# A graph attention layer and a normalised adjacency layer on one core: panel loads out of the attention, two panels' sums beside the first layer, and two re-orderings

## The reference, cut to what matters

```python
# x: 2048 x 512 f32, adj: 2048 x 2048 f32 of zeros and ones, H = 16 heads of 32
seq = (x @ W_seq).reshape(N, H, DH)
score1, score2 = einsum('nhd,d->hn', seq, a1), einsum('nhd,d->hn', seq, a2)
scores = leaky_relu(score1[:, :, None] + score2[:, None, :], 0.2) + (1 - adj) * -65500.0
hidden = einsum('hij,jhd->ihd', softmax(scores), seq).reshape(N, D)
x = layernorm(x + elu(hidden @ W_out + b_out))          # first layer
A = (adj + adj.T) * 0.5 + I;  d = rowsum(A) ** -0.5
y = (adj @ (d[:, None] * A * d[None, :])) @ x
x = layernorm(x + y)                                     # second layer
```

## Time and profile before

| | |
|---|---|
| median of three runs | 788.12 us (787.64 to 789.85) |
| profiled execution, its own time | 786.61 us |
| span of the profiled execution | 784.8 us |
| mean granted TensorE clock | 0.992 |
| TensorE busy | 749.7 us, 96% |
| VectorE, ScalarE, GpSimd busy | 554.7, 409.9, 130.1 us |
| attention, first matmul to last | 88.3 to 489.7 us |
| first layer, to the last `y_part` | 489.7 to 583.5 us |
| `y_product` | 583.5 to 666.4 us |
| `o_product` and end | 668.5 to 784.8 us |

### The profile page before, as it was taken

How to read it: one execution, slowest core, us unless ns; L and a number is a source line. 1 busy time by engine, 2 the same in 40 slices (tenths; PEclk the granted TensorE clock), 3 DMA queues, 4 the chain that set the end, 5 groups by cost and what they waited for, 6 DMA issues and landing times.

```text
span 784.8 us, 29353 instructions
## 1 busy us (share of the span) xinstructions
PE 749.7 (96%) x13731; PEld 552.4 (70%) x13731; DVE 554.7 (71%) x799; ACT 409.9 (52%) x302; POOL 130.1 (17%) x142
## 2 busy tenths in 40 slices
PE   6999799988999999999999999999999999999997
PEld 2444699988999999999999999444434444444443
DVE  2887899998988999999999983687772211333233
ACT  2874887986977888788897880333321111000000
POOL 0000113012320211101111001364433100000000
PEclk9999799999999999999999999999999999999999
DMA  7992510255313111011110121599119800001111
GB/s 304 413 406 103 235 57 5 84 110 110 56 60 84 58 58 36 26 58 58 58 58 4 58 71 31 97 186 175 54 31 172 119 0 1 18 36 41 41 40 41
DMA packets 17770, 71.65 MB, mean 91 GB/s; under 512 B 2016, under 2 KB 2016, under 8 KB 13408
## 3 DMA queue, kind: packets, MB, share of 16 engines
q1 hardware_dynamic: 13040, 52.99, 17.7%
q0 software_dynamic: 4608, 16.78, 14.1%
HBM read 77.89 MB, written 8.65 MB: 110 GB/s over the span
## 4 chain that ended last, share of the span: by engine, by line
PE 78%; DVE 15%; issue 5%; ACT 1%; DMA 1%; POOL 0%; DVEq 0%; POOLq 0%; SPq 0%; ACTq 0%
PE bank L631 13%; PE bank L534 12%; PE bank L533 12%; PE bank L531 11%; PE bank L618 11%; PE bank L467 7%; PE bank L579 7%; DVE RZ L852 5%; PE bank L587 3%; DVE RG L871 2%; DVE RG L867 2%; DVE RP L816 1%; PE bank L571 1%; DVE MT L892 1%; DMA RZ<-in_L_gnn_W_seq_dram 1%
## 5 line engine op out<-in xcount | busy, mean ns | idle before, releaser
L531 PE MATMUL bank<-RP,RG 128*128 128x66 f16 x4096 | 388.8, 193 | 6.9 <-DVE RG L871 3.6
L534 PE MATMUL bank<-RP,MT 128*128 128x66 f16 x4096 | 388.7, 194 | 3.6 <-issue 3.6
L531 PEld LDWEIGHTS bank<-RP,RG 128*128 128x128 fp8e4 x4096 | 386.3, 98 | 8.3 <-DVE RG L871 3.6
L533 PE MATMUL bank<-RP,RG 128*128 128x66 f16 x4096 | 388.7, 195 | 2.1 <-issue 2.1
L534 PEld LDWEIGHTS bank<-RP,MT 128*128 128x128 fp8e4 x4096 | 386.4, 98 | 3.2 <-issue 3.2
L533 PEld LDWEIGHTS bank<-RP,RG 128*128 128x128 fp8e4 x4096 | 386.4, 97 | 2.7 <-issue 2.7
L689 ACT ACTIVATE RZ<-RZ,TAB 128x2048 int8<-128x2048 f32 x160 | 306.6, 1988 | 15.3 <-DVE RG L867 14.5
L852 DVE TENSOR_SCALAR RZ<-RZ,TAB 128x2048 int8<-128x2048 f32 x96 | 132.3, 1378 | 0.0
L867 DVE TENSOR_TENSOR RG<-RZ,MT 128x512 int32<-128x512 int32 x160 | 121.7, 760 | 0.1
L631 PE MATMUL bank<-RZ,MT 128*128 128x512 f16 x512 | 110.7, 379 | 2.2 <-DVE MT L1023 2.2
L391 POOL TENSOR_TENSOR RP<-SEQ,TAB 128x528 f32<-128x528 f32 x32 | 52.2, 1652 | 331.8 <-DVE RP L818 256.7
(11 more groups left out here) (103 smaller groups left out, 593.2 us busy)
## 6 DMA issues: line engine op xcount, KB each, us to landing
RG<-in_adj_t_dram SPq DMA_DIRECT2D x16, 1024.0 KB, 10.6
RZ<-s_rows_dram SPq DMA_DIRECT2D x16, 1024.0 KB, 5.8
seq_copy_dram<-SEQ SPq DMA_DIRECT2D x1, 4224.0 KB, 14.2
S2Q<-in_adj_p_dram POOLq DMA_DIRECT2D x8, 512.0 KB, 6.3
S2Q<-in_adj_tp_dram POOLq DMA_DIRECT2D x8, 512.0 KB, 11.3
RZ<-in_x_dram SPq DMA_DIRECT2D x16, 256.0 KB, 3.5
RP<-in_adj_p_dram POOLq DMA_DIRECT2D x8, 512.0 KB, 7.1
RP<-in_adj_tp_dram POOLq DMA_DIRECT2D x8, 512.0 KB, 13.8
```

What stands on the lines that cost most here:

```text
L531: mm(pb[bank][:, c:c + 2 * DV], step, high, start=(j == 0 and i % IB == 0), stop=(j == NT - 1), skip_group_check=True)
L533: mm(pb[bank][:, c:c + 2 * DV], step, low, start=False, stop=(j == NT - 1), skip_group_check=True)
L534: last = mm(pb[bank][:, c + DV:c + 3 * DV], mask, edge, start=False, stop=(j == NT - 1), skip_group_check=True)
```

## The change

`NE` = 2 panels' sums are made beside the first layer, not `NQ` = 4; their transfers are issued when TensorE is two tiles from the end of the last head. No panel is loaded during the attention. The other fourteen panels go through `y_product`. Panels 2 to 9 are loaded from GpSimd's first-layer loop. The broadcast of score1 comes in `NS` = 4 pieces, each when the same quarter of the masks of the head before is made. `take_back` goes ahead of `low_z`. The first two output tiles leave the products with the last tile of z until both have done the other fifteen.

```diff
-            with sp.Fori(1, H // 2) as p:
-                for u in range(2):
-                    h = p * 2 + u
-                    sp.wait_ge(z_ready, h * NV - NV)
-                    sp.wait_ge(g_ready, h * NT - NT)
-                    load_s1(h, u)
+            def load_s1(h, q):
+                i = slice(q * (N // NS), (q + 1) * (N // NS))
+                sp.dma_start(S1B[:, h % 2, i], s1_rows[h:h + 1, i].broadcast_to([P, N // NS])).then_inc(s1b_in[h % 2], 16)
+            for h in range(2, H):
+                sp.wait_ge(z_ready, (h - 1) * NV)
+                for q in range(NS):
+                    sp.wait_ge(g_ready, (h - 1) * NT + q * (NT // NS))
+                    load_s1(h, q)
...
             for h in range(2, H):
                 prep(h)
-                if 3 <= h < 3 + NQ:
-                    load_panel(h - 3)
-                if 4 <= h < 4 + NQ:
-                    add_panel(h - 4)
-                if 5 <= h < 5 + NQ:
-                    add_diagonal(h - 5)
...
+            gp.wait_ge(g_used, NG + H * NT - 2)
+            for t in range(NE):
+                load_panel(t)
+            for t in range(NE):
+                add_panel(t)
             gp.wait_ge(att_end, 1)
             for t in range(NT):
-                if t < NP:
-                    load_panel(NQ + t)
-                if 2 <= t < 2 + NP:
-                    add_panel(NQ + t - 2)
-                if 4 <= t < 4 + NP:
-                    add_diagonal(NQ + t - 4)
+                if t + NE < NQ + NP:
+                    load_panel(t + NE)
+                if NE <= t < NQ + NP:
+                    add_panel(t)
+                if 2 <= t < 2 + NE:
+                    add_diagonal(t - 2)
+                if 3 + NE <= t < 3 + NQ + NP:
+                    add_diagonal(t - 3)
                 rstd_of(t, var_done, rstd_done)
                 if t + 2 < NT:
                     x_minus_1(t + 2)
-            for t in range(NQ + NP, NT):
-                gp.wait_ge(y_ps, NQ if t < 2 * NQ + NP else t - NQ - NP + 1)
-                load_panel(t)
-            for t in range(NQ + NP, NT):
-                add_panel(t)
-            for t in range(NQ + NP, NT):
-                add_diagonal(t)
+            for t in range(NQ + NP, NT + 2):
+                if t < NT:
+                    gp.wait_ge(y_ps, t - NQ - NP + 1)
+                    load_panel(t)
+                if NQ + NP < t <= NT:
+                    add_panel(t - 1)
+                if NQ + NP + 1 < t:
+                    add_diagonal(t - 2)
...
-                for i in range(NQ):
+                for i in range(NE):          # y_part
...
-                    pe.wait_ge(s2_done, NQ)
+                    pe.wait_ge(s2_done, NE)
...
-            for t in range(NQ, NT):
+            for t in range(NE, NT):
                 y_product(t)
             pe.wait_ge(mt_back, NT)
-            for t in range(NT):
-                o_product(t)
+            for t in range(2):
+                o_product(t, range(NT - 1))
+            for t in range(2):
+                o_product(t, range(NT - 1, NT))
+            for t in range(2, NT):
+                o_product(t, range(NT))
...
             for t in range(NT):
+                take_back(t)
                 low_z(t)
-                take_back(t)
```

More of the change, by code:

```diff
@@ L44, in gat_then_normalised_adjacency @@
     NQ = 4
+    NE = 2
+    NS = 4
     NP = 6
@@ L317, in _ @@
             sp.wait_ge(s1_stored, 16)
-            def load_s1(h, u):
-                sp.dma_start(S1B[:, u, :], s1_rows[DS(h, 1), :].broadcast_to([P, N])).then_inc(s1b_in[u], 16)
+            def load_s1(h, q):
+                i = slice(q * (N // NS), (q + 1) * (N // NS))
+                sp.dma_start(S1B[:, h % 2, i], s1_rows[h:h + 1, i].broadcast_to([P, N // NS])).then_inc(s1b_in[h % 2], 16)
             sp.wait_ge(seq_ps, NT)
-            load_s1(0, 0)
-            load_s1(1, 1)
+            for q in range(NS):
+                load_s1(0, q)
+            for q in range(NS):
+                load_s1(1, q)
             sp.wait_ge(tabs_done, 1)
             sp.dma_start(seq_copy[:, :], SEQ[:, :, :, :].rearrange("p t h d -> p (t h d)")).then_inc(seq_stored, 16)
-            with sp.Fori(1, H // 2) as p:
-                for u in range(2):
-                    h = p * 2 + u
-                    sp.wait_ge(z_ready, h * NV - NV)
-                    sp.wait_ge(g_ready, h * NT - NT)
-                    load_s1(h, u)
+            for h in range(2, H):
+                sp.wait_ge(z_ready, (h - 1) * NV)
+                for q in range(NS):
+                    sp.wait_ge(g_ready, (h - 1) * NT + q * (NT // NS))
+                    load_s1(h, q)
             sp.wait_ge(z_ready, (H - 1) * NV)
@@ L620, in y_product, with o_product @@
                 last.then_inc(y_ps, 1)
-            def o_product(t):
-                if t < 8:
+            def o_product(t, js):
+                if js[0] == 0 and t < 8:
                     pe.wait_ge(yv_done, t + 9)
-                else:
+                elif js[0] == 0:
                     pe.wait_ge(ov_done, t - 7)
-                for j in range(NT):
+                for j in js:
                     if t == 0:
@@ L632, in o_product @@
                                   start=(j == 0 and l == 0), stop=(j == NT - 1 and l == 1))
-                last.then_inc(o2_ps, 1)
+                if js[-1] == NT - 1:
+                    last.then_inc(o2_ps, 1)
             pe.wait_ge(v_added, NT)
-            for t in range(NQ, NT):
+            for t in range(NE, NT):
                 y_product(t)
             pe.wait_ge(mt_back, NT)
-            for t in range(NT):
-                o_product(t)
+            for t in range(2):
[4 more added lines that the diff above has]
+                o_product(t, range(NT))
         @block.scalar
@@ L682, in att_head @@
                 u = h % 2
-                sc.wait_ge(s1b_in[u], (h - u) * 8 + 16)
+                sc.wait_ge(s1b_in[u], (h // 2 + 1) * 16 * NS)
                 for j in range(NT):
@@ L848, in att_head @@
                 u = h % 2
-                ve.wait_ge(s1b_in[u], (h - u) * 8 + 16)
+                ve.wait_ge(s1b_in[u], (h // 2 + 1) * 16 * NS)
                 def own_step(m):
```

## The result

| | before | after |
|---|---|---|
| median | 788.53 us (787.48 to 790.29, 20 runs) | 791.1 us (789.17 to 794.35, 20 runs) |
| profiled execution: span | 784.8 us | 789.5 us |
| first matmul of the attention | 88.36 us | 88.97 us |
| end of the attention (VectorE takes head 15 out) | 489.73 us | 480.67 us |
| stage of the first layer, from there to the first `y_product` | 93.8 us | 96.1 us |

The ratio is 1.0032 [1.0023, 1.0042]: 0.3% slower, where 0.4% faster was forecast. The two spans differ by 4.7 us: -9.1 (attention), +2.3 (stage), +13.8 (products), and -2.4 for the rest (-2.16 of it the gap). The forecast had -9.1, -5.8, +13.8 and -2.2. One step failed, by 8.1 us: the first-layer stage. Times by stage are from one profiled execution of each kernel; runs of the kernel after alone differ by up to 5.2 us, so a tenth of a microsecond in a stage isn't more than a reading of one trace.

The account below looks back on a forecast made before the run. TensorE was taken as the bound, with gaps in the attention put down to panel loads. Attention -9.1, pieces 0, first layer and products +8.0, order -2.2 gave -3.3 us: median 784.8 us, range 779.8 to 790.5.

Parts of the forecast that it names:

- Attention: Attention with no panels loaded: TensorE's gaps from 132.4 to 256.5 us close, -9.1 us (bounds 0 and -9.4).
- Pieces: Broadcast of score1 in four pieces: a quarter lands in 3 us, effect 0 (bounds -0.4 and +1 us).
- products: Two `y_product`s added after the first layer, 6.91 us each: +13.8 us.
- order at the end: Start of the output products: taking back moves into VectorE's idle time and the gap goes, -2.2 us.
- The stage: First layer, attention's end to first `y_product`: two panels' sums fewer, -5.8 us (bounds 0 and -10.6).
- The price of a panel with its x: DMA time in the first-layer loop: load 2.6, sum 3.7, x some 0.9 us, 7.2 us together.
- the calendar: First-layer times from the attention's end: sum 9 +74.9, `rstd_of(12)` +75.2, stage's end +88.3, 5.5 us earlier than +93.8.
- The stage's hidden length: First layer with everything else hidden: ends at +83.2 us rather than +93.8, -10.6 us.
- (c): Rival, first layer: sums come later still and the stage gains nothing, +2.5 us, 790.6 us; chance 0.12.
- (a): Rival, first layer: the panels' late sums are hidden, stage gains 10.6, -8.1 us in all, 780.0 us; chance 0.2.
- (b): Rival, attention: only half of the gaps close, -4.5 there, +1.3 us in all, 789.4 us; chance 0.15.
- (d): Rival, attention: gaps are not the DMA's doing and stay, +5.8 us, 793.9 us; chance 0.05.

Follow-up runs that it names:

- b_tail_order: Kernel before with only the new order at the start of the output products (take_back ahead of low_z): 785.92 us, 0.9957.
- g_x_four: Kernel after with four buffers of x instead of two, same loads, panels and bytes: 787.36 us, 0.9991.
- f_three_early: Kernel after with three panels in the first-layer loop, panels 0 and 1 asked for twelve tiles before the attention's end, not two: 782.92 us, 0.9932.
- d_both_pieces: Kernel before with the attention's four panels loaded in quarters over eleven heads (early places) and the broadcasts in quarters: 784.07 us, 0.9961.
- d_panel_pieces: Kernel before with the attention's four panels loaded in quarters over eleven heads (early places), broadcasts whole: 790.3 us, 1.0008.

## Why the prediction was wrong, by its steps

**Attention, right.** -9.1 forecast and measured, though to the tenth that is luck: in the window that the forecast was read from the gaps fell by 8.4 us, and the attention as a whole is 9.7 us shorter and began 0.6 us later. The reason given, instruction packets late behind full DMA engines, agrees with the packet times; no run moved the packets alone. The Trainium skill, "Runtime: NRT & Kernel Launch", section "Instruction fetch mechanics", has the fetch in blocks of 16 KB, as these packets are, and "mostly hidden". This trace agrees from 256.5 to 449 us, where there is no gap, and not from 132.4 to 256.5 us, where 8.35 us of gaps stand behind late packets.

**Pieces, products, order at the end: right.** 0, +13.8 and -2.2; the lone -3.4 +- 1.3 of `b_tail_order` doesn't contradict it.

**The stage, wrong:** -5.8 forecast, +2.3 measured. The sentence that failed first is "it waits for each sum before `rstd_of`" as the gate, since GpSimd waited 3.1 us for sums in the loop and 14.3 for x; and the one that cost most is "VectorE then has tiles 14 and 15: 4.0 us", since from x - 1 of tile 14 to tile 15 VectorE took 7.0 us. From the end of the attention:

| | forecast | after | `g_x_four` |
|---|---|---|---|
| sum of panel 9 | +74.9 | +78.2 | +75.65 |
| `rstd_of(12)` | +75.2 | +78.55 | +76.2 |
| first ELU step of tile 15 | +80.8 | +87.6 | +85.2 |
| first `y_product` | +88.3 | +96.1 | +93.7 |

*3.35 us before `rstd_of(12)`.* The price of a panel with its x, 7.2 us, was good: with the x buffers doubled, sum 9 is 0.75 us off. But x had been charged as 0.9 us of bandwidth only, a term for which no row was given. It is also a small load that somebody waits for: VectorE frees one of two buffers, SyncE loads it, GpSimd adds -1, VectorE uses it. Before, that circle mostly closed in time. Over the fourteen loads of x from 490 us to the stage's end the median to landing was 4.2 us, over the first thirteen 5.5:

```profile
RZ<-in_x_dram SPq DMA_DIRECT2D x13, 256.0 KB, 5.5
```

After, it is 7.7 for the fourteen, GpSimd stands at line 422 for 14.3 us (before: 5.5), and its list is in order, so loads and sums behind it start later still. The same circle, with panel 2's load at 487.31 ahead of x in the engines, made the diagonals of panels 0 and 1 late for `y_part(0)`: 2.62 us. With three panels that wait isn't there.

*3.4 us from there to tile 15.* At +80.55 x - 1 of tile 14 was done, but VectorE began tile 14 (its line 1008) only 2.5 us later, since it still had the rest of tile 13; this I had left out:

```profile
558.98 0.83 DVE L1008 SCALAR_TENSOR_TENSOR RZ<-RZ 128x512 f32<-128x512 f32 x1 [1.58 <-POOL RZ L422]
...
563.69 0.69 DVE L1008 SCALAR_TENSOR_TENSOR RZ<-RZ 128x512 f32<-128x512 f32 x1
...
568.26 0.69 DVE L1008 SCALAR_TENSOR_TENSOR RZ<-RZ 128x512 f32<-128x512 f32 x1
```

And a tile took it 4.57 us, not 4.0: line 1014 (1018 in `g_x_four`), begun at 560.33 and at 564.90, takes 1.45 us; in the kernel before the same step, line 1003, took 0.68 in the last tiles. The remaining 0.4 us is in GpSimd's `rstd_of(12)` and `x - 1`, 2.0 us together where 1.6 had been taken. In the two tiles line 422 runs on GpSimd beside line 1014. In the same run line 1014 took 0.68 to 0.78 us in the thirteen tiles in which it had at most 0.3 us of line 422 beside it, and where line 422 fell on line 1000, at 550.48, that one took 1.52 instead of some 0.75. The Trainium skill, "SBUF — State Buffer", section "SBUF: two separate sides", says that an operation of VectorE with two SBUF inputs and one of GpSimd that reads SBUF lock each other out of a shared port pair; these durations agree with that, though no run here took `x - 1` away from GpSimd to test it.

*1.0 us at the end.* The sixteen matmuls of the last `y_part`s took 6.39 us. The windows: TensorE had been busy for 4.72 of 10 us, and the granted clock is 0.58 behind it, mostly the lower level, 1.2 GHz:

```profile
560.00:570.00 10.00, 4.72 (x15) 1.65 (x13) 9.90 (x18) 2.70 (x4) 4.12 (x5) 0.95 0.08 26
...
570.40:576.80 6.40, 6.30 (x17) 1.99 (x18) 4.45 (x9) 1.79 (x3) 1.13 (x2) 0.58 0.00 0
```

At the 0.216 us of a full clock they are 3.5 us, so I put 2.9 down to the clock; most of it lies under VectorE's last steps.

The three make 7.8; the other 0.3 is that the calendar gave -5.5 and I took -5.8. The stage's hidden length, 83.6 measured, was right within half a microsecond. Both can be so because without lateness TensorE, at 4.74 us a tile, stays the slower one up to its last product, and VectorE's 4.57 costs nothing. What the forecast missed in general: with these two paces lateness in the loop is hardly made up any more. Before, TensorE's pace was 5.60, and VectorE could gain a microsecond a tile.

**The rivals.** (c) had the place and, at 790.6, nearly the time, but by another road: by its rule, a microsecond of the stage for each of sum 9, the stage would be 91.6 us. (a), the sums hidden in the loop, 780.0 us, is what happens with three panels: 779.73. (b) and (d) fall with the windows of the attention.

**Left open.** How the 2.4 us of x's circle and the clock's part divide in a run with both; why `f_three_early`'s first layer is also 1.8 us longer.

## What to carry to other kernels

A transfer moved beside another stage costs more than its bytes: list the small loads that an in-order engine waits for there, take their landing time beside full engines (here 7.7 us, not 2.6), and add it to their circle. Then ask at what pace the next engine could make lateness up. Here it was within 0.2 us a tile of the bound, so lateness stayed to the end, and fewer transfers (three panels instead of eight, 0.9889) beat more.

## What was unexpected of the hardware

TensorE, at 24.06 us for 768 matmuls with their weight loads, takes a 16 KB instruction packet every 3.4 to 4.5 us, and in the kernel before had a gap of 1.13 us or more behind each of the six that came 5.6 to 7.1 us after the last. That is no fixed limit: `d_both_pieces` has a gap of 1.03 us behind an interval of 5.04. A 1 MB broadcast alone was enough where it began just before a packet was due (6.45 us, gap 0.85), and made no gap where it began beside one. So spreading the same panels in small transfers over more heads opened gaps where there had been none: 8.4 us of them in `d_panel_pieces`.
